# Sums of the message layer with nodes on the partitions, and a rectifier taken inside an addition

## The chip, the cores and the metric

The kernel runs on one core of one Trainium2 chip. The metric is the device time of one execution in microseconds (us); smaller is better. Runs of the kernel before and of the changed kernel are compared by their medians.

The engines of a core are named as in the profile: PE is TensorE (matrix products), PEld its weight loads, DVE is VectorE, ACT is ScalarE, POOL is GpSimd, SP is SyncE, which here only issues DMA transfers.

## What is computed

A graph transformer layer over 1250 nodes with 512 features and 21250 edges. Its branches are a graph message layer, linear attention and a feed-forward part with eight experts. The change touches the message layer, in the reference:

```python
m = jnp.maximum(jnp.max(weighting_gate), jnp.float32(0.0))
exp_e = jnp.exp(weighting_gate - m)
row_sum = jax.ops.segment_sum(exp_e, src, num_segments=n_nodes)
atten_e = exp_e / (row_sum[src] + 1e-06)
Mfeat = source_features @ Wm + bm
out0 = jax.ops.segment_sum(atten_e[:, None] * Mfeat[dst], src, num_segments=n_nodes)
out1 = jax.ops.segment_sum(atten_e[:, None] * Mfeat[src], dst, num_segments=n_nodes)
message_feats = jnp.concatenate([out0, out1], axis=-1)
h = message_feats @ W1 + b1
h = jax.nn.relu(_layernorm(h, gamma, beta))
h = jax.nn.relu(h @ W2 + b2)
valid = (row_sum > 0)[:, None]
return jnp.where(valid, h, jnp.float32(0.0))
```

and around it:

```python
xn = _layernorm(x, axis=-1)
x = x + gnn(xn, ...) + mix(xn[None], ...)[0]
x = x + ffn(_layernorm(x, axis=-1)[None], ...)[0]
```

## The kernel before

The 1250 nodes are 10 tiles of 125 nodes (`NT`, `TP`); two tiles form a window of 250 nodes (`WIN`), of which there are five (`NW`). The program is written by hand for each engine: every engine has its own list of instructions and semaphores between them, and nothing reorders them.

The stages in order of time: loads and edge sorting beside the projections of all tiles (to about 150 us), attention output and more sorting (to 225 us), the dense weighted adjacency matrix built from the sorted edges (L731, L739 on PE, L1646 on ACT, to 312 us), the message layer (312.6 to some 392 us), routing to the experts (to 410 us), and 17 chunks of the expert layer (to the end).

Wm and W1 are folded ahead, so `msg` holds for each node 256 values: 128 for the sum outwards (columns 0 to GH) and 128 for the sum inwards (GH to MD), both of them already in the 128 features of h. `adjw` holds the adjacency in float32, node of a tile t on the partitions, the other node in windows along the free axis.

**First loop of the message layer** (t over 10 tiles). `adj_turn` turns the ten 125x125 blocks of tile t on PE (L751), ACT copies the result as the rounded part `adjT_hi` (L1654) and DVE takes the rest as `adjT_lo` (L1297). Then `inward(t)` (L758) adds, for each of the five windows, `msg[:, t, GH:MD]` (loaded as weights, 128 columns) times `adjw` (streamed, 250 columns) into `hid_at(w)`. These are float32 products. The result stands with the 128 features on the partitions and nodes along the free axis.

**Second loop** (w over 5 windows). `outward(w, half)` (L781 to L783) adds for each of ten source tiles j three products in the type float32r: `out_hi` or `out_lo` as weights (128 columns), 250 columns of `adjT_hi` or `adjT_lo` streamed, into `hid_to(w)`. ACT copies both sums to SBUF (`hid_in` L1667, with the bias b1, and `hid_copy` L1675), PE turns them so that nodes are on the partitions (`hid_turn`, L793 and L794), and DVE scales the outward part with 1/row_sum and adds the inward part (`hid_var`, L1323 and L1326), takes mean and variance, and normalises (`hid_norm`, L1343). PE turns the result back (`hid_back`, L802), ACT applies gamma, beta and the rectifier (L1686), PE multiplies with W2 (`hid_out`, L809, one product for each tile), DVE adds b2 (`upd_bias`, L1351), ACT applies the rectifier and the mask of valid nodes (`relu`, L1691), DVE adds the result to the residual stream `rec` (`x1_norm`, L1356) and takes its statistics. PE turns `rec` (`x2_turn`, L817), ACT copies it (L1697), PE computes the router's scores (`route`, L824, 8 columns streamed).

In each list the steps of different windows are interleaved by hand. DVE's list after the first loop is, for w from 1 to 7: `hid_var(w-1)`, `x1_norm`, `hid_norm(w-1)`, `x1_norm`, two `upd_bias`; so the sums of the last window stand behind `upd_bias` of tiles 4 and 5 there.

SP waits for the last outward sum (`hid_ps`), then issues in this order: four pieces of the experts' second weights (L462, 1 MB each), half of the first weights (L463, 2 MB), their bias (L464, 2 MB), the ten tiles of `rec` as they become ready (L398, 2.56 MB in all) and last the factors of every row (L470). POOL gathers the rows for the experts (L507) after all of that has been written.

Of the kernel before, what the change touches and what calls it, by code (L numbers as in the profile page):

```python
# [13 lines left out]
ALU = mybir.AluOpType  # L14
# [20 lines left out]
WIN = 250  # L35
# [76 lines left out]
def build(nc, x, edge_src, edge_dst, edge_w, consts, halves, biases, small, fold, wqkv, wp, bvt, w1f, w2f, b2f, out):  # L112
    with ExitStack() as ctx:
# [107 lines left out]
        hidc = place("hidc", 26064, [128, 2, WIN])  # L221
        hido = place("hido", 40664, [128, 2, WIN])
# [49 lines left out]
        valid = sb("valid", [TP, NT])  # L272
# [36 lines left out]
        def hid_at(w):  # L309

            return bank[3 + w][:, 0:WIN]

        def hid_to(w):

            return bank[3 + w][:, 256:256 + WIN]
# [9 lines left out]
        def piece(a, i):  # L325
# [51 lines left out]
        hidi_ok, comb_ok = sem("hidi_ok"), sem("comb_ok")  # L377
        hid_ps, hidc_ok, hn_ps, hvar_ok, hstd_ok, hn_ok, hT_ps, hidT_ok, upd_ps, upd_ok, relu_ok, x1_ok = (
            sem("hid_ps"), sem("hidc_ok"), sem("hn_ps"), sem("hvar_ok"), sem("hstd_ok"), sem("hn_ok"), sem("hT_ps"),
            sem("hidT_ok"), sem("upd_ps"), sem("upd_ok"), sem("relu_ok"), sem("x1_ok"))  # L380
# [35 lines left out]
        def _(sp):  # L416
# [43 lines left out]
            sp.wait_ge(hid_ps, NW)  # L460
            for i in range(4):
                sp.dma_start(piece(w2_raw, i), piece(w2f, i)).then_inc(ld_w2k[i], 16)  # L462
# [63 lines left out]
        def _(pe):  # L526
# [1333 lines left out]
```

## Time and profile before

| | us |
|---|---|
| median of 3 runs | 494.15 (493.7 to 494.18) |
| the profiled execution, its time | 493.5 |
| the profiled execution, first to last instruction (span) | 491.4 |
| first loop of the message layer | 312.6 to 344.7 |
| second loop up to the last outward sum | 344.7 to 371.6 |
| from there to the first gather of the experts' rows | 371.6 to 405.5 |

Over the whole span PE is busy for 86%, its weight loads for 70%, DVE 75%, ACT 61%, POOL 40%; the mean granted clock of PE is 0.959 of full speed. Of the chain that ended last, PE has 64% of the span.

How to read it: times in the trace are us from the first instruction. In a row of instructions the name before the arrow is written, those after it are read (streamed operand first, loaded weights second), then rows and columns of the weights, then rows and columns streamed. A float32 product that is no turn leaves two records, one for each pass over its columns; a turn and a float32r product leave one (both types are shown as f32). Records of PE overlap, so what one costs in a stream is the distance between two starts, or the time of a group in the chain of work divided by its count; the mean ns of one is its latency.

### The profile page before, as it was taken

How to read it: one execution, taken by the hardware profiler on the slowest of the kernel's cores; microseconds unless marked ns; L12 is line 12 of the kernel's file. 1: busy time of each engine (PE TensorE's matmuls, PEld its weight loads, DVE VectorE, ACT ScalarE, POOL GpSimd, SP SyncE). 2: the span in 40 equal slices, each digit the busy share in tenths (PEclk: the TensorE clock that was granted, in tenths of full speed). 3: DMA queues.
4: the chain of work that ended last, by engine and by line, in shares of the span. 5: the costliest groups of instructions: out<-in, count | busy, mean ns of one | idle time of the engine just before them, and what ended most of it. 6: DMA issues, size and time to landing. Idle time of an engine off the chain costs nothing.

```text
span 491.4 us, 8811 instructions
## 1 busy us (share of the span) xinstructions
PE 424.5 (86%) x2701; PEld 343.4 (70%) x2701; DVE 366.9 (75%) x717; ACT 298.3 (61%) x845; POOL 194.8 (40%) x160
## 2 busy tenths in 40 slices
PE   3665999999999999999777777899898957999992
PEld 1454887888887788877555555799876746788881
DVE  6786688877786888698999998478279874455552
ACT  4577999988897123363777777554335662666550
POOL 0378878688887787870000000000000008254321
PEclk9878999999999999999999999999999858999998
DMA  7992000000000000005000000000006964243210
GB/s 228 284 250 49 1 3 3 1 4 2 3 3 1 2 2 3 2 3 191 2 1 2 1 2 0 3 1 0 1 1 258 412 225 128 74 120 110 68 65 16
DMA packets 15742, 31.07 MB, mean 63 GB/s; under 512 B 7652, under 2 KB 8283, under 8 KB 14675
## 3 DMA queue, kind: packets, MB, share of 16 engines
q1 hardware_dynamic: 9266, 23.21, 14.6%
q0 software_dynamic: 6432, 7.31, 7.5%
q8 instruction: 24, 0.39, 0.3%
q14 instruction: 20, 0.16, 0.1%
HBM read 24.90 MB, written 7.37 MB: 66 GB/s over the span
## 4 chain that ended last, share of the span: by engine, by line
PE 64%; ACT 14%; DVE 10%; issue 6%; DMA 3%; POOL 1%; SPq 1%; ACTq 0%; DVEq 0%; POOLq 0%
PE banks L569 25%; PE banks L739 9%; PE banks L892 7%; PE banks L758 4%; ACT adj L1646 4%; PE banks L751 2%; ACT q_sb L1580 2%; PE banks L824 2%; PE banks L650 2%; PE banks L883 2%; ACT k_sb L1580 1%; DVE chunk_1h L1214 1%; DMA x_rows<-factors 1%; ACT q_sb L1563 1%; PE banks L731 1%
## 5 line engine op out<-in xcount | busy, mean ns | idle before, releaser
L496 POOL DMA_INDIRECT slots<-record,row_i x116 | 153.7, 1325 | 40.7 <-issue 40.7
L507 POOL DMA_INDIRECT rec<-x_rows,get_i x17 | 18.7, 1098 | 190.7 <-DMA x_rows<-factors 185.8
L1646 ACT ACTIVATE adj<-banks x108 | 58.4, 588 | 27.9 <-PE banks L739 26.8
L569 PE MATMUL banks<-w_hi,xT_hi 128*125 128x512 f32 (+1 forms) x160 | 61.5, 385 | 5.7 <-DVE xT_lo L1085 5.7
L739 PE MATMUL banks<-d_hot,s_hot 128*128 128x251 f16 x432 | 60.0, 276 | 0.2
L569 PE MATMUL banks<-w_lo,xT_hi 128*125 128x512 f32 (+1 forms) x160 | 60.1, 375 | 0.0
L569 PE MATMUL banks<-w_hi,xT_lo 128*125 128x512 f32 (+1 forms) x160 | 60.0, 375 | 0.0
L569 PEld LDWEIGHTS banks<-w_hi,xT_hi 128*125 128x125 f32 x160 | 30.9, 193 | 12.0 <-issue 6.1
L739 PEld LDWEIGHTS banks<-d_hot,s_hot 128*128 128x128 f16 x432 | 33.5, 98 | 7.5 <-issue 0.7
L569 PEld LDWEIGHTS banks<-w_lo,xT_hi 128*125 128x125 f32 x160 | 30.9, 193 | 5.8
L569 PEld LDWEIGHTS banks<-w_hi,xT_lo 128*125 128x125 f32 x160 | 30.6, 191 | 6.1
L516 POOL DMA_INDIRECT out<-o_sb,out_i x17 | 17.1, 1005 | 40.9 <-DVE o_sb L1462 40.9
L1268 DVE TENSOR_TENSOR d_hot<-col,keys 128x2000 f16<-128x2000 f16 (+1 forms) x28 | 32.3, 1153 | 0.0
L731 PE MATMUL banks<-hlf 128*128 128x1 f16 x108 | 18.3, 170 | 16.1 <-ACT adj L1646 16.1
L1276 DVE TENSOR_TENSOR s_hot<-s_one,parts 128x2048 f16<-128x2048 f16 x26 | 31.6, 1215 | 0.0
L1457 DVE TENSOR_TENSOR y_sb<-banks,b_sb 128x512 f32<-128x512 f32 x17 | 11.8, 691 | 26.2 <-PE banks L569 26.2
L731 PEld LDWEIGHTS banks<-hlf 128*128 128x128 f16 x108 | 10.4, 96 | 28.9 <-issue 26.9
L1580 ACT ACTIVATE q_sb<-q_sb,hmax 125x64 f32<-125x64 f32 x80 | 26.7, 335 | 4.3 <-DVE hmax L1113 4.2
L1609 ACT ACTIVATE row_1h<-row_one,sort_f 125x128 f16<-125x128 f16 x54 | 19.7, 432 | 13.8 <-DVE row_one L1208 8.0
L1580 ACT ACTIVATE k_sb<-k_sb,hmax 125x64 f32<-125x64 f32 x80 | 26.6, 333 | 0.0
L702 PE MATMUL banks<-chunk_1h,row_1h 125*128 125x216 f16 x216 | 22.8, 258 | 3.2 <-DVE chunk_1h L1214 2.2
L1617 ACT ACTIVATE xT_hi<-banks 128x500 fp32r<-128x500 f32 x10 | 5.9, 588 | 30.6 <-PE banks L663 30.6
(297 smaller groups left out, 1083.1 us busy)
## 6 DMA issues: line engine op xcount, KB each, us to landing
w_raw<-in_w2f SPq DMA_DIRECT2D x4, 1024.0 KB, 8.1
w_raw<-in_wqkv SPq DMA_DIRECT2D x3, 1024.0 KB, 15.2
x_rows<-rec SPq DMA_DIRECT2D x10, 224.0 KB
w1a<-in_w1f SPq DMA_DIRECT2D x1, 2048.0 KB, 7.8
w1b<-in_w1f SPq DMA_DIRECT2D x1, 2048.0 KB, 16.5
b_sb<-in_b2f SPq DMA_DIRECT2D x1, 2048.0 KB, 22.9
slots<-record,row_i POOLq DMA_INDIRECT x116, 2.6
rec<-in_x SPq DMA_DIRECT2D x1, 1120.0 KB
```

Source lines behind the costliest of these rows:

```text
L496: pool.indirect_dma_start(slots, bass.IndirectOffsetOnAxis(ap=row_i[:, c:c + 1], axis=0), record[:, c, :], None).then_inc(slot_st, 16)
L569: mm = pe.matmul(dst, ab, cd, start=(i == 0), stop=(i == n - 1))
L702: mm = pe.matmul(bank[1 - v // 2][:, v % 2 * NCH:(v % 2 + 1) * NCH], row_1h[:, n % RS, v, :, j], chunk_1h[:, n % RS, :, j], start=(n == 0 ...
L731: pe.matmul(flat_banks[:, bass.ds(at_new, 1)], before, zero_col, start=True, stop=False, skip_group_check=True)
L739: mm = pe.matmul(flat_banks[:, bass.ds(at_in, AW)], s_hot[:, n % DB, i, q, :, j], d_hot[:, n % DB, q, :, j], start=False, stop=(i == WT - ...
L758: mm = pe.matmul(hid_at(w), msg[:, t, GH:MD], adjw[:, t, w, 0:WIN], start=(t == 0), stop=(t == NT - 1), skip_group_check=True)
L892: mm = pe.matmul(bank[1][:, 0:F], xsT[:, c % 2, k, :], w1_sb[k // 2][:, k % 2, bass.ds(e * F, F)], start=(k == 0), stop=(k == KD - 1))
L1268: dve.tensor_tensor(d_hot[:, r, 0:k, 0:WIN, :], col_2[:, :, :].unsqueeze(1).to_broadcast([128, k, WIN, 2]), of_keys(1).to_broadcast([128, ...
L1276: last = dve.tensor_tensor(s_hot[:, r, :, :, :, :], s_one[:, n % 2, :, :, :].unsqueeze(1).to_broadcast(shape), both.unsqueeze(3).to_broadc ...
L1580: last = act.activation(ah, ah, ACT.Exp, bias=hmax[:, i, h:h + 1], accum_out=hsum[:, i, h:h + 1])
L1609: last = act.activation(row_1h[:, n % RS, VD, :, j], row_one[:, n % 2, :, j], ACT.Copy, scale=sort_f[:, 2 * n + j:2 * n + j + 1])
L1646: act.activation(adj[:, bass.ds(w, BW2)], flat_banks[0:TP, bass.ds(out_at, BW2)], ACT.Copy).then_inc(win_ok, 1)
```

## The change

The operands of the two sums change places. The adjacency blocks are loaded as weights (125 columns) and the 128 features of the messages are streamed, so the sums stand with nodes on the partitions. Their copies in that layout (`hidc`, `hido`) and the turns of `hid_turn` go. The bias b1, which stood on the partitions, is put in by ten small products at the start of the first loop (`in_bias`: b1 spread over 125 weight columns, the identity streamed). DVE takes the outward sum straight from PSUM, scales it and adds the inward sum in one instruction for each tile; the inward sums are copied by ACT to a new tile `hin`. `hin` lies where the second and third quarter of the experts' second weights are to go, so SP waits for the last use of it before pieces 1 to 3. The mask of valid nodes becomes an addend (0, or -3e38 for a node that is not valid) in `upd_bias`, and the rectifier is taken by DVE as a maximum with 0 in the addition to `rec`; ACT's `relu` goes.

```diff
@@ tiles and places in PSUM
-        hidc = place("hidc", 26064, [128, 2, WIN])
-        hido = place("hido", 40664, [128, 2, WIN])
+        hin = place("hin", 10240, [TP, NW, 2, GH])
-        def hid_at(w):
-            return bank[3 + w][:, 0:WIN]
-        def hid_to(w):
-            return bank[3 + w][:, 256:256 + WIN]
+        def in_at_of(n):
+            return bank[3 + n // 2][0:TP, n % 2 * MD:n % 2 * MD + GH]
+        def out_at_of(n):
+            return bank[3 + n // 2 if n >= 2 else 0][0:TP, n % 2 * MD + GH:(n % 2 + 1) * MD]
@@ SP
-            sp.wait_ge(hid_ps, NW)
+            sp.wait_ge(hid_ps, NT)
             for i in range(4):
+                if i == 1:
+                    sp.wait_ge(comb_ok, NW)
                 sp.dma_start(piece(w2_raw, i), piece(w2f, i)).then_inc(ld_w2k[i], 16)
@@ PE
+            def in_bias(n):
+                pe.matmul(in_at_of(n), little("g1").to_broadcast([128, TP]), ident, start=(n % 2 == 0), stop=False,
+                          skip_group_check=True)
             def inward(t):
-                for w in range(NW):
-                    mm = pe.matmul(hid_at(w), msg[:, t, GH:MD], adjw[:, t, w, 0:WIN], start=(t == 0),
-                                   stop=(t == NT - 1), skip_group_check=True)
+                for n in range(NT):
+                    mm = pe.matmul(in_at_of(n), adjw[:, t, n // 2, n % 2 * TP:(n % 2 + 1) * TP], msg[:, t, GH:MD],
+                                   start=False, stop=(t == NT - 1), skip_group_check=True)
...
+                if t == 0:
+                    pe.wait_ge(ld_small, 16)
+                    for n in range(NT):
+                        in_bias(n)
...
-            def outward(w, half_):
-                if w >= 1 and half_ == 0:
-                    pe.wait_ge(hidi_ok, w)
-                for j in range(5 * half_, 5 * half_ + 5):
-                    cols = slice(w * WIN, (w + 1) * WIN)
-                    pe.matmul(hid_to(w), out_hi[:, j, :], adjT_hi[:, j, cols], start=False, stop=False, skip_group_check=True)
-                    pe.matmul(hid_to(w), out_hi[:, j, :], adjT_lo[w][:, j, :], start=False, stop=False, skip_group_check=True)
-                    mm = pe.matmul(hid_to(w), out_lo[:, j, 0:GH], adjT_hi[:, j, cols], start=False,
-                                   stop=(j == NT - 1), skip_group_check=True)
+            def outward(n):
+                cols = slice(n * TP, (n + 1) * TP)
+                if n >= 2:
+                    pe.wait_ge(hin_ok, n // 2 + 1)
+                low = slice(n % 2 * TP, (n % 2 + 1) * TP)
+                for j in range(NT):
+                    pe.matmul(out_at_of(n), adjT_hi[:, j, cols], out_hi[:, j, :], start=(n == 0 and j == 0), stop=False, skip_group_check=True)
+                    pe.matmul(out_at_of(n), adjT_hi[:, j, cols], out_lo[:, j, 0:GH], start=False, stop=False,
+                              skip_group_check=True)
+                    mm = pe.matmul(out_at_of(n), adjT_lo[n // 2][:, j, low], out_hi[:, j, :], start=False,
+                                   stop=(j == NT - 1), skip_group_check=True)
...
-            def hid_turn(w):
...
@@ DVE
-            dve.tensor_scalar(valid[:, :], rs[:, :], 0.0, None, ALU.is_gt)
+            dve.tensor_scalar(shut[:, :], rs[:, :], 0.0, -3e38, ALU.is_le, ALU.mult)
             def hid_var(w):
-                dve.wait_ge(hn_ps, w + 1)
+                dve.wait_ge(hid_ps, 2 * w + 2)
+                dve.wait_ge(hin_ok, w + 1)
                 for i in range(2):
-                    t = 2 * w + i
-                    last = dve.tensor_scalar(comb[:, w % 2, i, :], bank[0][0:TP, (2 + i) * GH:(3 + i) * GH], rinv[:, t:t + 1], None,
-                                             ALU.mult)
-                own_step(last)
-                dve.tensor_tensor(comb[:, w % 2, :, :], comb[:, w % 2, :, :],
-                                  bank[0][0:TP, 0:2 * GH].rearrange("p (i n) -> p i n", i=2), ALU.add).then_inc(comb_ok, 1)
+                    n = 2 * w + i
+                    last = dve.scalar_tensor_tensor(comb[:, w % 2, i, :], out_at_of(n), rinv[:, n:n + 1], hin[:, w, i, :], ALU.mult,
+                                                    ALU.add)
+                last.then_inc(comb_ok, 1)
...
-                dve.tensor_tensor(upd[:, t % 2, :], upd_at(t), bias("g2"), ALU.add).then_inc(upd_ok, 1)
+                dve.scalar_tensor_tensor(upd[:, t % 2, :], upd_at(t), shut[:, t:t + 1], bias("g2"), ALU.add,
+                                         ALU.add).then_inc(upd_ok, 1)
...
-                dve.wait_ge(relu_ok, t + 1)
-                dve.tensor_tensor(rec[:, t, :], rec[:, t, :], upd[:, t % 2, :], ALU.add).then_inc(x1_ok, 1)
+                dve.wait_ge(upd_ok, t + 1)
+                dve.scalar_tensor_tensor(rec[:, t, :], upd[:, t % 2, :], 0.0, rec[:, t, :], ALU.max,
+                                         ALU.add).then_inc(x1_ok, 1)
@@ ACT: hid_copy and relu go, and
             act.wait_ge(in_ps, 1)
-            hid_in(1).then_inc(hidi_ok, 1)
-            hid_copy(0)
+            for w in range(NW):
+                hid_in(w)
```

On PE the first loop stood like this before (turns L751, inward sums L758; `cst` is the table with the identity):

```order
L751 MATMUL banks<-cst,adj 125x125 x10
L758 MATMUL banks<-adj,msg 128x250 x5
L751 MATMUL banks<-cst,adj 125x125 x10
L758 MATMUL banks<-adj,msg 128x250 x5
```

and stands like this now (turns L752, bias L758, inward sums L764):

```order
L752 MATMUL banks<-cst,adj 125x125 x10
L758 MATMUL banks<-cst,sml 125x128 x10
L764 MATMUL banks<-msg,adj 125x128 x10
L752 MATMUL banks<-cst,adj 125x125 x10
L764 MATMUL banks<-msg,adj 125x128 x10
```

Each tile has ten inward products instead of five, and the first tile ten for the bias ahead of them.

At the end of the second loop on PE, before: the last outward products of window 4, then the products with W2 for tiles 4 and 5 (L809), the turn back (L802), the turns of `hid_turn` for window 4, and the scores of tiles 0 and 1 (L824).

```order
L781 MATMUL banks<-adjT_hi,out_hi 128x250
L782 MATMUL banks<-adjT_lo_90,out_hi 128x250
L783 MATMUL banks<-adjT_hi,out_lo 128x250
L809 MATMUL banks<-sml,hidT 125x512 x2
L802 MATMUL banks<-cst,hid 128x125 x2
L793 MATMUL banks<-cst,hidc 125x128
L794 MATMUL banks<-cst,hido 125x128
L793 MATMUL banks<-cst,hidc 125x128
L794 MATMUL banks<-cst,hido 125x128
L824 MATMUL banks<-sml,x2T 125x8 x8
```

Now, at the same place (outward products L792, L793, L795; the product with W2 is L811, the turn back L804, the scores L826):

```order
L792 MATMUL banks<-out_hi,adjT_hi 125x128
L793 MATMUL banks<-out_lo,adjT_hi 125x128
L795 MATMUL banks<-out_hi,adjT_lo_90 125x128
L811 MATMUL banks<-sml,hidT 125x512 x2
L804 MATMUL banks<-cst,hid 128x125 x2
L826 MATMUL banks<-sml,x2T 125x8 x8
```

The triples of outward products were 50 in all and are now 100; the turns are gone, and what follows keeps its order.

On SP, with what each transfer waits for, before:

```order
L462 DMA w_raw<-in_w2f 128x2048 [waits hid_ps]
L462 DMA w_raw<-in_w2f 128x2048 x3
L463 DMA w1b<-in_w1f 128x4096
L464 DMA b_sb<-in_b2f 128x4096
```

and now:

```order
L463 DMA w_raw<-in_w2f 128x2048 [waits hid_ps]
L463 DMA w_raw<-in_w2f 128x2048 [waits comb_ok]
L463 DMA w_raw<-in_w2f 128x2048 x2
L464 DMA w1b<-in_w1f 128x4096
L465 DMA b_sb<-in_b2f 128x4096
```

The second piece, and with it all that SP issues after it, now waits for `comb_ok`, which DVE raises with the sums of the last window.

## Rows read from the trace of the kernel before

**Rows 1.** Busy time by stage: us, busy us (instructions) by engine, clock, DMA share, GB/s.

```profile
312.60:344.70 32.10, 32.08 (x201) 29.93 (x201) 25.14 (x50) 14.54 (x31) 0.00 (x0) 1.00 0.00 1
344.70:371.60 26.90, 24.77 (x191) 22.22 (x190) 15.45 (x49) 10.84 (x23) 0.00 (x0) 1.00 0.01 1
...
374.80:400.50 25.70, 20.05 (x127) 16.23 (x126) 21.50 (x61) 15.63 (x22) 0.00 (x0) 0.78 1.02 398
```

**Rows 2.** Chain that ended last, first loop: start us, us, engine, line, count.

```profile
316.10 1.09 PE banks L751 x10
317.19 2.12 PE banks L758 x10
```

**Rows 3.** Timelines of PE and DVE, second loop: start, latency, instruction, count, [idle before].

```profile
345.17 0.28 PE L781 MATMUL banks<-adjT_hi,out_hi 125*128 125x250 f32 x1
...
350.06 0.27 PE L793 MATMUL banks<-cst,hidc 128*125 128x128 f32 x1
...
350.77 0.61 DVE L1323 TENSOR_SCALAR comb<-banks,rinv 125x128 f32<-125x128 f32 x2 [5.72 <-PE banks L794]
...
353.86 0.43 PE L802 MATMUL banks<-cst,hid 125*128 125x125 f32 x2 [1.45 <-DVE hid L1343]
...
366.52 0.43 PE L802 MATMUL banks<-cst,hid 125*128 125x125 f32 x2 [0.68 <-DVE hid L1343]
```

**Rows 4.** SP issuing the second weights; then their times to landing (L462).

```profile
371.78 1.98 SPq L462 DMA_DIRECT2D w_raw<-in_w2f  x4
...
DMA to landing us min/median/max: 5.0/8.1/11.1
```

**Rows 5.** Stages of 1 us; columns as in rows 1.

```profile
382.00:383.00 1.00, 1.00 (x9) 1.00 (x9) 0.81 (x3) 0.86 (x2) 0.00 (x0) 0.71 1.00 426
...
400.00:401.00 1.00, 0.00 (x0) 0.00 (x0) 0.90 (x5) 1.00 (x2) 0.00 (x0) 0.50 0.79 229
```

**Rows 6.** Chain of work behind the routing.

```profile
398.25 6.43 DMA x_rows<-factors
...
405.47 4.23 DMA rec<-x_rows,get_i
```

**Rows 7.** Timelines of PE and DVE around and behind the last outward sum.

```profile
369.19 0.61 DVE L1323 TENSOR_SCALAR comb<-banks,rinv 125x128 f32<-125x128 f32 x2
...
371.58 1.88 PE L809 MATMUL banks<-sml,hidT 128*125 128x512 f32 x4
...
374.72 1.27 DVE L1351 TENSOR_TENSOR upd<-banks,bia 125x512 f32<-125x512 f32 x2
375.91 0.60 DVE L1323 TENSOR_SCALAR comb<-banks,rinv 125x128 f32<-125x128 f32 x2
376.54 0.42 DVE L1326 TENSOR_TENSOR comb<-comb,banks 125x256 f32<-125x256 f32 x1
...
380.03 0.43 PE L802 MATMUL banks<-cst,hid 125*128 125x125 f32 x2 [1.57 <-DVE hid L1343]
```

**Rows 8.** Chain of work: scores of two tiles, twice; turns of an expert chunk.

```profile
380.46 1.65 PE banks L824 x16
...
392.30 3.24 PE banks L824 x16
...
424.24 0.44 PE banks L883 x4
```

**Rows 9.** Groups by line and shape, 310 to 420 us: busy us, mean ns | idle before.

```profile
L758 PEld LDWEIGHTS banks<-adj,msg 125*128 125x128 f32 x100 | 18.2, 190 | 1.7
...
L781 PEld LDWEIGHTS banks<-adjT_hi,out_hi 125*128 125x128 f32 x50 | 9.4, 189 | 0.0
```

**Rows 10.** Timeline of PE in the attention part.

```profile
59.99 0.69 PE L604 MATMUL banks<-v_sb,k_sb 125*64 125x65 f32 x16
60.61 0.65 PE L560 MATMUL banks<-cst,xn 125*128 125x125 f32 x4
```

More of the change, by code:

```diff
@@ L271, in build @@
         rinv = sb("rinv", [TP, NT])
-        valid = sb("valid", [TP, NT])
+        shut = sb("shut", [TP, NT])
         ws_sum = sb("ws_sum", [TP, E])
@@ L376, in build @@
             sem("out_split"))
[L377 to L380, printed above, removed]
+        hin_ok, comb_ok = sem("hin_ok"), sem("comb_ok")
+        hid_ps, hvar_ok, hstd_ok, hn_ok, hT_ps, hidT_ok, upd_ps, upd_ok, x1_ok = (
+            sem("hid_ps"), sem("hvar_ok"), sem("hstd_ok"), sem("hn_ok"), sem("hT_ps"),
+            sem("hidT_ok"), sem("upd_ps"), sem("upd_ok"), sem("x1_ok"))
         var2_ok, std2_ok, x2T_ps, x2T_ok, log_ps, log_ok, lexp_ok, route_ok, route_ps = (
@@ L773, in _ @@
             ws = little("ws").rearrange("p (k e) -> p k e", k=KD)
[L775 to L795 removed]
+            def outward(n):
[8 more added lines that the diff above has]
+                    mm = pe.matmul(out_at_of(n), adjT_lo[n // 2][:, j, low], out_hi[:, j, :], start=False,
+                                   stop=(j == NT - 1), skip_group_check=True)
+                mm.then_inc(hid_ps, 1)
             def hid_back(w):
@@ L835, in _ @@
             for w in range(NW):
-                outward(w, 0)
-                if w >= 1:
-                    hid_turn(w - 1)
+                outward(2 * w)
                 if w == NW - 1:
                     both(x2_turn, 0)
-                outward(w, 1)
+                outward(2 * w + 1)
                 if w >= 2:
@@ L845, in _ @@
                     hid_back(w - 1)
-            hid_turn(NW - 1)
             both(route, 0)
@@ L1664, in hid_in @@
             def hid_in(w):
-                if w >= 2:
-                    act.wait_ge(hn_ps, w - 1)
-                return act.activation(hidc[:, w % 2, :], hid_at(w), ACT.Identity, bias=little("g1"))
-            def hid_copy(w):
-                act.wait_ge(hid_ps, w + 1)
-                if w == 0:
-                    hid_in(0)
-                if w >= 2:
-                    act.wait_ge(hn_ps, w - 1)
-                act.activation(hido[:, w % 2, :], hid_to(w), ACT.Copy).then_inc(hidc_ok, 1)
+                act.activation(hin[:, w, :, :], bank[3 + w][0:TP, :].rearrange("p (i a) -> p i a", i=2)[:, :, 0:GH],
+                               ACT.Copy).then_inc(hin_ok, 1)
             def hid_std(w):
@@ L1687, in hid_relu @@
                                scale=little("gamma")).then_inc(hidT_ok, 1)
-            def relu(t):
-                act.wait_ge(upd_ok, t + 1)
-                act.activation(upd[:, t % 2, :], upd[:, t % 2, :], ACT.Relu, scale=valid[:, t:t + 1]).then_inc(relu_ok, 1)
             def x2_copy(t):
@@ L1709, in _ @@
             act.wait_ge(in_ps, 1)
-            hid_in(1).then_inc(hidi_ok, 1)
-            hid_copy(0)
+            for w in range(NW):
+                hid_in(w)
             for w in range(1, NW):
-                if w + 1 < NW:
-                    hid_in(w + 1).then_inc(hidi_ok, 1)
                 if w == NW - 1:
@@ L1717, in _ @@
                 hid_std(w - 1)
-                hid_copy(w)
                 if w == NW - 1:
                     hid_relu(w - 1)
-                if w >= 2:
-                    both(relu, w - 2)
                 if w < NW - 1:
@@ L1727, in _ @@
             hid_relu(NW - 1)
-            both(relu, NW - 2)
             both(x2_copy, 2)
-            both(relu, NW - 1)
             both(x2_copy, 3)
```

9 lines of the change are left out of this document (removed).

## The prediction, made before the changed kernel ran

> **What bounds the kernel now.** I read the busy time by stage first. In the first loop of the message layer PE is busy 32.08 of 32.10 us, in the second 24.77 of 26.90 us up to the last outward sum; DVE has 25.14 and 15.45 us there, ACT 14.54 and 10.84 [rows 1]. So PE sets both loops, and a nanosecond added to each product is paid in full. Then the chain that ended last: one tile of the first loop is 1.09 us of turns and 2.12 us of inward sums, ten times over, with nothing between [rows 2]. Then PE's timeline in the second loop: from 345.17 to 350.06 there are 42 outward products, so they start 0.1165 us apart, and all 150 take 17.5 us; PE idles twice for DVE, 1.45 and 0.68 us [rows 3].
>
> Behind the last outward sum another thing rules. At 371.78 SP begins to issue the experts' weights [rows 4], and from then on the DMA engines carry some 11 MB (8 MB of weights and bias, 2.56 MB of rows): from 374.8 to 400.5 their share is 1.02, at 398 GB/s [rows 1]. The stream thins out only after 400 [rows 5]. The factors are issued at 398.25, stand behind it, and land 6.43 us later; the gather and the expert layer start from there [rows 6]. So this part ends not when DVE and PE have the routing, but when the stream that began at the last outward sum has drained. DVE and PE have about 2 us to spare.
>
> **The change part by part.** T is the end of the last outward product on PE, 371.58 before [rows 7].
>
> *Inward sums.* Per tile 5 x 250 streamed columns become 10 x 128, in two passes each. Before, ten records took 2.12 us, 0.212 each; by columns a pass over 128 is 0.109 [rows 2]. Four turns over 128 columns took 0.44 us, 0.110 each [rows 8]. Twenty passes at 0.110 are 2.2 us, 0.08 more for each tile: +0.8 us.
>
> *Bias.* Ten products of 128 columns in two passes, 20 x 0.110 = +2.2 us. They stand on PE between turns and sums of the first tile, in a loop where PE never waits [rows 1], so nothing hides them.
>
> *Outward sums.* This is the large term. 150 products that stream 250 columns become 300 that stream 128. The streamed columns stay the same but for 2%, yet every product has its own weight load, and the number of loads doubles. The trace shows a load for each record even where the weights repeat: L758 uses one block of weights for five windows and has 100 loads for its 100 records [rows 9]. How fast can loads follow one another? The scores (L824) load 125 columns for every 8 streamed: 16 in 1.65 us, 0.103 each [rows 8]; nothing but the load can take that. The turns of the first loop load the very adjacency blocks and stream 125 columns: 0.109 each [rows 2], so load and stream overlap. The load for a float32r product has the latency of one for float32, 189 and 190 ns [rows 9], so I take it to be the same work. The new products stream for some 0.06 us (128/250 of 0.1165) under a load of 0.103. I put them between 0.103 and 0.109, at 0.106: 300 x 0.106 = 31.8 us against 17.5, +14.3 us. Ends of the unknown: 0.163 (0.103 + 0.060) if load and stream of short float32r products do not overlap; 0.076 if loads are as quick as the attention's products with 64 weight columns suggest, 16 in 0.62 us or 0.038 each, doubled [rows 10]; 0.060 if only the stream counted.
>
> *Turns.* 16 of the 20 turns of `hid_turn` stand before T: four groups like the 0.44 us of rows 8, -1.75 us. The last group is off the path.
>
> *Stalls.* PE's waits of 1.45 and 0.68 us are for `hid_norm` [rows 3]. A window now takes PE at least 60 x 0.106 = 6.4 us, while the way from sums to `hid_norm` took 353.86 - 350.77 = 3.1 us. They go, -2.1 us. Next late would be DVE, whose round for a window took 375.91 - 369.19 = 6.7 us [rows 7], and which saves 0.4 us of it (two instructions of 0.3 for 0.60 and 0.42). PE has 6.4 us of sums, 1.7 of products with W2 (L809) and 0.2 of turns in each round, so it is never behind DVE.
>
> *ACT.* Five copies of 256 columns come in a row after the first loop; DVE's instruction of that size takes 0.42 us [rows 7], so ACT's may take as much, 2 us in all. PE needs them only for the third outward tile, 6.4 us later. Nil. The removed copies and `relu` stood beside PE's work, and behind T in the slack named above. Nil.
>
> *The new wait on SP.* Pieces 1 to 3, and all that SP issues behind them, wait for DVE's sums of the last window. In DVE's list `upd_bias` of tiles 4 and 5 stands ahead, and that needs L809, which PE makes right after T: 1.88 us, then 0.64 for the second `upd_bias` and 0.60 for the two sums [rows 7]. That makes T + 3.2; SP issues at T + 3.4 instead of T + 0.7. Meanwhile piece 0 occupies the DMA engines. The first piece landed 5.0 us after its issue, the last, issued some 1.6 us later, 11.1 us after its own [rows 4]: 2.5 us for each. Piece 1 landed near T + 7.7 and can now land at T + 3.4 + 5.0 = T + 8.4. So the stream is late by 0.7 us; by 0 if piece 1 starts up wholly under piece 0, by 2.7 us if nothing hides. I take +0.7, nearest to the landing times.
>
> *Routing.* DVE reaches the last window's sums at T + 2.6 instead of T + 4.3 [rows 7] and is 2 to 3 us nearer to T with the factors. By the stream that is worth nothing. The clock fell to half after 382 [rows 5], and of two equal groups of scores the one at 392.30 took 3.24 us instead of 1.65 [rows 8]; that too lies in the slack. If this slack were not there, up to 2 us would be gained.
>
> Sum: 0.8 + 2.2 + 14.3 - 1.75 - 2.1 + 0.7 = +14.15 us. On the profiled execution's 493.5 that gives 507.65; the median of the runs stands 0.65 above it, so 508.3.
>
> **A rule against this, weighed.** The chain shows 0.103 for a load with 8 streamed columns [rows 8]. The Trainium skill, "TensorE: Matmul & The Clock Gate", section "Back-to-back issue gap", gives about 81 ns for each product of a stream of loads and products at 128 columns. By it the outward sums would take an estimated 24.3 us and the total would be near 500.8. For this type the trace disagrees. The same page, Part 3, says that a load overlaps a running product only when their row groups differ; here they would then not overlap, which is the third rival below. The 0.109 of a turn that both loads and streams 125 columns [rows 2] disagrees with that as well.
>
> **Rivals.**
> *Quicker loads.* 0.076 each, 9 us less: 499.3. For it: L604's 0.038 for 64 columns [rows 10]. Against: those products write the two halves of the array in turn and may overlap each other, and the scores' weights have the same shape as the new ones.
> *No slower than before.* If loads cost nothing and only the stream counted, PE would pay 0.0595 x 300 = 17.9 us for the outward sums, and 0.8 + 2.2 + 0.4 - 1.75 - 2.1 + 0.7 = +0.25; with 128 columns at the rate of a float32 pass (0.109 for two columns' time each, 0.055) it is 16.4 us and -1.3: 492.9. The time turns at 0.0587 for a product. Against it stands every row with a load in it, and PE's stalls would stay, with windows as short as before.
> *No overlap.* 0.163 each, 17.1 us more: 525.4. For it: no row shows float32r with so short a stream. Against: the turns.
> *Clock.* PE streams for only half of the outward stage. If the granted clock fell to 1.2 GHz as it did behind 382 [rows 5], a load would take twice as long, as in rows 8: +31.8, 540. Against: that fall came behind 1.57 us of idle [rows 7] and behind scores that stream only 8 columns; here there is neither.
>
> **How the numbers follow.** Forecast 0.71, its own spread 505 to 512.5 (0.103 to 0.116 for a product, 0 to 2.7 for the stream). Quicker loads 0.10 (499 to 505), no slower than before 0.06, no overlap 0.07, clock 0.04, rest 0.02. The range holds the first two: 499 to 512.5. A measurement of this kernel tells about 0.2% (1 us) from no change: faster 0.04, within that 0.02, slower 0.94.
>
> **What would show it.** In the profile after: a first loop 3.0 us longer, 3.29 us a tile; outward products 0.106 us apart at full clock; no idle of PE for DVE before T; T near 385; the last window's sums done 3.2 us behind T; the gather again behind the factors' landing, whose issue has moved nearer to T while the landing has not; nothing changed from the gather to the end. A distance of 0.08 or 0.16 between outward starts would make the forecast wrong, and so would a gather much nearer to T than 34.6 us (405.47 - 371.58 [rows 6, 7], plus 0.7).

## The result, and the profile after

| | kernel before | changed kernel |
|---|---|---|
| median, 4 runs each | 493.92 us (492.47 to 494.18) | 508.56 us (506.73 to 511.79) |
| profiled execution: time | 493.5 | 509.01 |
| span | 491.4 | 506.9 |

The ratio is 1.0312, 95% interval 1.0278 to 1.0346: 14.6 us slower by the medians. The forecast was 508.3, range 499 to 512.5, so time, direction and size came as forecast. What follows is whether they came for the reasons given.

The versions further down ran on other chips, each beside runs of the kernel before (medians 495.26, 492.9 and 493.28 us), and their ratios are to those. Executions in a slower state, such as one of the last version with 595.35 us at a mean granted clock of 0.682, count in no ratio.

First the busy time by stage of the changed kernel (us; then busy us and count of PE, PEld, DVE, ACT, POOL; granted clock; DMA share; GB/s). The stages are the first loop, the second loop to the last outward sum (T), and T to the gather.

```profile
312.70:347.90 35.20, 35.20 (x323) 35.20 (x323) 25.48 (x50) 14.54 (x31) 0.00 (x0) 1.00 0.00 1
347.90:385.30 37.40, 37.40 (x323) 35.37 (x321) 16.84 (x52) 6.59 (x15) 0.00 (x0) 1.00 0.01 1
385.30:420.10 34.80, 28.31 (x169) 23.19 (x169) 30.61 (x77) 15.99 (x20) 0.01 (x1) 0.75 0.85 316
```

Against [rows 1] PE is now busy for all of both loops, its loads for nearly all, and its clock is full. The chain of work shows the first loop (start, us, count): the bias, then 1.09 and 2.19 us for a tile, where [rows 2] has 1.09 and 2.12.

```profile
314.02 2.19 PE banks L758 x20
316.20 2.19 PE banks L764 x20
318.39 1.09 PE banks L752 x10
319.48 2.19 PE banks L764 x20
```

PE's timeline in the second loop, where [rows 3] has products every 0.1165 us (column two is a record's latency):

```profile
347.98 0.27 PE L792 MATMUL banks<-out_hi,adjT_hi 125*125 125x128 f32 x1
348.09 0.27 PE L793 MATMUL banks<-out_lo,adjT_hi 125*125 125x128 f32 x1
...
350.27 0.28 PE L792 MATMUL banks<-out_hi,adjT_hi 125*125 125x128 f32 x1
```

21 products stand between 347.98 and 350.27: 0.109 each, 32.8 us for 300. The groups by line and shape show a load for every record, of the same latency as before [rows 9]:

```profile
L792 PEld LDWEIGHTS banks<-out_hi,adjT_hi 125*125 125x125 f32 x100 | 18.9, 189 | 0.0
```

Behind T, SP's timeline with its four pieces of the stream:

```profile
385.49 4.36 SPq L463 DMA_DIRECT2D w_raw<-in_w2f  x4
```

and DVE's timeline:

```profile
386.41 1.61 DVE L1349 SCALAR_TENSOR_TENSOR upd<-banks,shut,bia 125x512 f32<-125x512 f32 x2 [0.94 <-PE banks L811]
387.93 0.60 DVE L1323 SCALAR_TENSOR_TENSOR comb<-banks,rinv,hin 125x128 f32<-125x128 f32 x2
```

DVE's last window sums end at 388.53, 3.2 us behind T, and SP's four pieces stretch over 4.36 us instead of 1.98 [rows 4]. The chain then, where [rows 6] has 6.43 us and the gather at 405.47:

```profile
412.50 6.82 DMA x_rows<-factors
...
420.09 4.08 DMA rec<-x_rows,get_i
```

So the profiled spans differ like this (T is 371.58 and 385.30):

| stretch | before | after | difference | forecast |
|---|---|---|---|---|
| start to first loop | 312.62 | 312.69 | +0.1 | 0 |
| first loop | 32.4 | 35.2 | +2.8 | +3.0 |
| second loop to T | 26.6 | 37.4 | +10.8 | +10.45 |
| T to the gather | 33.9 | 34.8 | +0.9 | +0.7 |
| gather to the end | 85.9 | 86.8 | +0.9 | 0 |
| sum | 491.4 | 506.9 | +15.5 | +14.15 |

One sign came otherwise than forecast: the factors are issued 27.2 us behind T (412.50) and not nearer to it than before (398.25, 26.7 us behind). The section on SP's wait comes back to it.

### The profile page after: what moved, and what is told of

It is laid out like the page before. It is cut to its first block, busy times and chain, and to the rows that moved or that the text cites. A ratio compares the mean times of both kernels' runs of the same rounds, so it can differ in the third digit from the quotient of the medians.

```text
span 506.9 us, 9288 instructions
## 1 busy us (share of the span) xinstructions
PE 439.8 (87%) x2951; PEld 361.0 (71%) x2951; DVE 365.7 (72%) x712; ACT 290.0 (57%) x830; POOL 192.6 (38%) x160
## 4 chain that ended last, share of the span: by engine, by line
PE 66%; ACT 13%; issue 6%; DVE 5%; SPq 4%; DMA 3%; POOL 1%; ACTq 0%; DVEq 0%; POOLq 0%
PE banks L570 24%; PE banks L740 9%; PE banks L891 6%; PE banks L764 4%; SPq L397 4%; ACT adj L1646 4%; PE banks L752 2%; PE banks L793 2%; PE banks L795 2%; PE banks L792 2%; ACT q_sb L1580 2%; PE banks L882 2%; PE banks L651 2%; ACT k_sb L1580 1%; DMA x_rows<-factors 1%
## 5 line engine op out<-in xcount | busy, mean ns | idle before, releaser
L508 POOL DMA_INDIRECT rec<-x_rows,get_i x17 | 17.0, 998 | 205.3 <-DMA x_rows<-factors 200.4
L1646 ACT ACTIVATE adj<-banks x108 | 58.5, 589 | 27.8 <-PE banks L740 26.7
L570 PEld LDWEIGHTS banks<-w_hi,xT_hi 128*125 128x125 f32 x160 | 30.6, 191 | 14.5 <-issue 8.6
L740 PEld LDWEIGHTS banks<-d_hot,s_hot 128*128 128x128 f16 x432 | 33.5, 98 | 7.5 <-issue 0.7
L570 PEld LDWEIGHTS banks<-w_hi,xT_lo 128*125 128x125 f32 x160 | 30.4, 190 | 6.0
L1457 DVE TENSOR_TENSOR y_sb<-banks,b_sb 128x512 f32<-128x512 f32 x17 | 11.8, 692 | 26.7 <-PE banks L570 26.7
L1580 ACT ACTIVATE q_sb<-q_sb,hmax 125x64 f32<-125x64 f32 x80 | 26.7, 336 | 4.3 <-DVE hmax L1112 4.2
L792 PE MATMUL banks<-out_hi,adjT_hi 125*125 125x128 f32 x100 | 27.4, 274 | 0.0
L795 PE MATMUL banks<-out_hi,adjT_lo 125*125 125x128 f32 x100 | 27.2, 272 | 0.0
L793 PE MATMUL banks<-out_lo,adjT_hi 125*125 125x128 f32 x100 | 27.2, 272 | 0.0
## 6 DMA issues: line engine op xcount, KB each, us to landing
w1b<-in_w1f SPq DMA_DIRECT2D x1, 2048.0 KB, 14.5
```

The costliest lines, as they stand in the source:

```text
L570: mm = pe.matmul(dst, ab, cd, start=(i == 0), stop=(i == n - 1))
L740: mm = pe.matmul(flat_banks[:, bass.ds(at_in, AW)], s_hot[:, n % DB, i, q, :, j], d_hot[:, n % DB, q, :, j], start=False, stop=(i == WT - ...
L792: pe.matmul(out_at_of(n), adjT_hi[:, j, cols], out_hi[:, j, :], start=(n == 0 and j == 0), stop=False, skip_group_check=True)
L793: pe.matmul(out_at_of(n), adjT_hi[:, j, cols], out_lo[:, j, 0:GH], start=False, stop=False, skip_group_check=True)
L795: mm = pe.matmul(out_at_of(n), adjT_lo[n // 2][:, j, low], out_hi[:, j, :], start=False, stop=(j == NT - 1), skip_group_check=True)
L1580: last = act.activation(ah, ah, ACT.Exp, bias=hmax[:, i, h:h + 1], accum_out=hsum[:, i, h:h + 1])
```

## What sets the distance of the outward products

The theory is that the weight load sets it; its rival, that the short float32r stream does. Two versions of the changed kernel halve one of the two. The first leaves out the outward sums of the nodes 64 to 124 of each tile:

```diff
-                cols = slice(n * TP, (n + 1) * TP)
+                cols = slice(n * TP, n * TP + 64)
-                low = slice(n % 2 * TP, (n % 2 + 1) * TP)
+                low = slice(n % 2 * TP, n % 2 * TP + 64)
-                    pe.matmul(out_at_of(n), adjT_hi[:, j, cols], out_hi[:, j, :], ...
+                    pe.matmul(out_at_of(n)[0:64, :], adjT_hi[:, j, cols], out_hi[:, j, :], ...
```

and the same for the other two products.

> The changed kernel, with only 64 of the 125 weight columns loaded in each outward product (the outward sums of the nodes 64 to 124 of each tile are left out); 128 columns are still streamed. The outward products started 0.109 us apart in the changed kernel. Theory (the load sets this distance): 64 columns load in about half the time, so the starts come down to 0.06 to 0.08 us, and 300 products are 9 to 15 us shorter: 494 to 500 us. Rival (the stream sets it, float32r streaming 128 columns at the rate of a float32 pass, 0.109): the distance stays 0.109 and the time stays near 508.5.

PE's timeline:

```profile
350.51 0.22 PE L792 MATMUL banks<-out_hi,adjT_hi 125*64 125x128 f32 x1
...
352.32 0.22 PE L792 MATMUL banks<-out_hi,adjT_hi 125*64 125x128 f32 x1
```

30 products lie between these two rows, 0.060 us each. With half the weight columns and all 128 columns streamed the distance falls from 0.109 to 0.060. So the load set it, and a float32r stream of 128 columns takes 0.060 or less. That is close to the break-even of the prediction, 0.0587, and from the first loop to SP's first piece this kernel takes 58.4 us (313.7 to 372.05), the kernel before 59.2. The time is 498.09 us, 1.0059 of the kernel before (1.0011 to 1.0106): what it loses lies behind that point (35.6 us to the gather and 88.5 to the end, for 33.7 and 85.9), where other sums are routed. That wasn't followed up.

The second version leaves out half of the features of the outward sums:

```diff
-                    pe.matmul(out_at_of(n), adjT_hi[:, j, cols], out_hi[:, j, :], ...
+                    pe.matmul(out_at_of(n)[:, 0:64], adjT_hi[:, j, cols], out_hi[:, j, 0:64], ...
```

> The changed kernel, with only 64 of the 128 columns streamed in each outward product (half of the features of the outward sums are left out); 125 weight columns are loaded as before. Theory (load sets the distance): 0.103 to 0.109 us between starts, at most 2 us less in all, 506.5 to 508.5. Rival (the stream sets it): the stream is halved, and the distance would fall to the load's 0.103 as well if load and stream overlap, so this run alone does not part the two; but if load and stream were served one after the other (0.109 = load + part of the stream), it would fall below 0.09 and the time below 503.

Neither came: 538.54 us. PE's timeline, and the stages around the place (columns as above):

```profile
354.55 0.27 PE L795 MATMUL banks<-out_hi,adjT_lo 125*125 125x64 f32 x1
354.66 0.27 PE L792 MATMUL banks<-out_hi,adjT_hi 125*125 125x64 f32 x1
354.77 0.31 PE L793 MATMUL banks<-out_lo,adjT_hi 125*125 125x64 f32 x1
354.89 0.40 PE L795 MATMUL banks<-out_hi,adjT_lo 125*125 125x64 f32 x1
355.10 0.40 PE L792 MATMUL banks<-out_hi,adjT_hi 125*125 125x64 f32 x1
355.31 0.40 PE L793 MATMUL banks<-out_lo,adjT_hi 125*125 125x64 f32 x1
```

```profile
350.00:354.00 4.00, 4.00 (x39) 4.00 (x39) 0.65 (x2) 2.77 (x6) 0.00 (x0) 1.00 0.02 4
354.00:356.00 2.00, 2.00 (x16) 2.00 (x15) 0.00 (x0) 0.00 (x0) 0.00 (x0) 0.72 0.00 0
356.00:380.00 24.00, 24.00 (x116) 24.00 (x116) 4.23 (x18) 1.15 (x3) 0.00 (x0) 0.50 0.00 1
```

Up to 354.8 the products stand 0.109 us apart (14 of them from 353.24 to 354.77), with half the stream: the load again, and not load and stream one after the other. Then the granted clock falls to 1.2 GHz and the distance becomes 0.21. PE is busy without a gap, and so are its loads; what is less than in the changed kernel is only the columns streamed. This is what the prediction's fourth rival, given 0.04 and priced with +31.8, had feared. The version takes 30 us more than the changed kernel, 24.5 of them from the first loop to SP's first piece (97.3 us for 72.8); with 128 columns the fall doesn't happen.

## The bias products

```diff
-                if t == 0:
-                    pe.wait_ge(ld_small, 16)
-                    for n in range(NT):
-                        in_bias(n)
...
-                                   start=False, stop=(t == NT - 1), ...
+                                   start=(t == 0 and n % 2 == 0), stop=(t == NT - 1), ...
```

> The changed kernel without the ten bias products (the bias b1 is left out); the first inward product of each bank starts the sum. Theory: they stand uncovered on PE, 2.2 us; the first loop and the whole are 2.2 us shorter, 506.3. Rival (the wait for the first scaled messages stands behind them and takes their place): at most 0.5 us is gained, 508.

Measured 508.98 us, ratio to before 1.0289 (1.0211 to 1.0367). The interval is wider than the effect, so the stage decides: from the first loop's start to SP's first piece 70.7 us (313.1 to 383.8) instead of 72.8. The 2.1 us are there and uncovered, though the whole doesn't show them. In its chain the inward sums follow the turns at once:

```profile
313.11 1.33 PE banks L752 x10
314.44 2.22 PE banks L764 x20
```

## What sets the gather

The prediction said that behind T the DMA stream is the bound, not routing. Three kernels tell that. The first loads 2 MB more:

```diff
             sp.dma_start(b2_sb[:, :], b2f.partition_broadcast(128)).then_inc(ld_b2, 16)
+            sp.dma_start(spare[:, :], b2f.partition_broadcast(128)).then_inc(ld_b2, 16)
```

> The kernel before with 2 MB more in the stream behind T (the experts' output bias is loaded a second time, into a region that is free then). Theory (the stream sets the gather): 2 MB at some 420 GB/s are 5 us, the gather comes 5 us later and the whole takes 499, up to 1 us more for a colder clock. Rival (routing sets it, the stream is cover): the first 2 us are free and the gather comes at most 3 us later, 497; if the stream had more slack, nothing changes.

498.29 us, ratio 1.0103 (1.0034 to 1.0172). From SP's first piece to the gather it takes 39.3 us (370.4 to 409.7) instead of 33.7: 2 MB cost 5.6 us in full. More of routing ran at half clock in this execution, so the factors were also issued later (30.0 us behind SP's first piece for 26.5); but the list of rows stood ready at 406.0, 3.7 us ahead of the gather. The factors took 8.50 us to land instead of 6.43. The stream is the bound, not routing.

The second takes the rectifier's part of the change alone, on the kernel before:

```diff
-                dve.tensor_tensor(upd[:, t % 2, :], upd_at(t), bias("g2"), ALU.add).then_inc(upd_ok, 1)
+                dve.scalar_tensor_tensor(upd[:, t % 2, :], upd_at(t), shut[:, t:t + 1], bias("g2"), ALU.add,
+                                         ALU.add).then_inc(upd_ok, 1)
...
-                dve.tensor_tensor(rec[:, t, :], rec[:, t, :], upd[:, t % 2, :], ALU.add).then_inc(x1_ok, 1)
+                dve.scalar_tensor_tensor(rec[:, t, :], upd[:, t % 2, :], 0.0, rec[:, t, :], ALU.max,
+                                         ALU.add).then_inc(x1_ok, 1)
```

> The kernel before with the second part of the change alone: mask as an addend, rectifier as a maximum in DVE's addition, no rectifier on ACT; the sums as before. Theory (behind T the DMA stream sets the end): T and the gather stay where they were, 0 within 0.5 us: 493.9. Rival (the chain over DVE and ACT sets it): two waits of 0.2 us and the hand-overs go, 1 to 2 us less, 492 to 493.

494.05 us, ratio 1.0016 (0.9979 to 1.0054): no change that can be told, with 33.5 us from SP's first piece to the gather, although the factors were written 1.2 us sooner against that piece. The rectifier's part of the change costs nothing that can be told; what the change costs comes with the new sums.

The third is the changed kernel with the load of the output bias issued behind the factors:

```diff
-            sp.dma_start(b2_sb[:, :], b2f.partition_broadcast(128)).then_inc(ld_b2, 16)
             for t in range(NT):
...
                          factors[:, :, :]).then_inc(fac_st, 16)
+            sp.dma_start(b2_sb[:, :], b2f.partition_broadcast(128)).then_inc(ld_b2, 16)
```

> The changed kernel with the load of the experts' output bias (2 MB) issued behind the factors instead of ahead of the rows. Theory: the stream ahead of the factors is 5 us shorter; the gather's list of rows is ready 5.3 us ahead of the gather in the changed kernel, so the gather comes nearly 5 us sooner. PE's warm-up products, which run until about 36 us behind T, then end behind it and hold back the first turns, so 3.5 of it are left: 505 (504 to 506). Rival (the rows' own small transfers set it, not the bytes ahead): no change, 508.5.

502.2 us, ratio to before 1.0168 (1.0111 to 1.0225), a larger gain than I had expected. The profile is of the slowest of the four executions (505.24 us). In it SP's first piece to gather is 31.3 us instead of 34.6. The list of rows is written at 417.1 and the gather starts at 418.1, so there routing has become the bound.

## What SP's new wait costs

Here the copies of the inward sums go where the inward half of the messages lies dead, and the wait goes.

```diff
-        hin = place("hin", 10240, [TP, NW, 2, GH])
-                if i == 1:
-                    sp.wait_ge(comb_ok, NW)
-                    ... rinv[:, n:n + 1], hin[:, w, i, :], ALU.mult,
+                    ... rinv[:, n:n + 1], msg[:, n, GH:MD], ALU.mult,
-                act.activation(hin[:, w, :, :], ...
+                act.activation(msg[:, 2 * w:2 * w + 2, GH:MD], ...
```

> The changed kernel with the copies of the inward sums written over the inward half of the messages, which is dead by then; SP's wait for the last window's sums goes. Theory: the stream of the experts' weights starts 0.9 us sooner against T and, since that stream sets when the gather starts, the gather comes 33.9 instead of 34.8 us behind T: 507.7. Rival (the stream makes a late start good, or something else sets the gather): the stretch from T to the gather stays 34.8 and the time 508.5.

510.73 us, ratio 1.0323 (1.0245 to 1.0401), no gain. SP's first piece to gather is 34.7 us, as long as with the wait. To see how steady this stretch is, both kernels were profiled again, unchanged.

> The kernel before, unchanged, for its stages on this chip: first loop to T 59.0 to 59.2 us, T to the gather 33.7 us. If the second stretch differs from 33.7 by half a microsecond, the 0.9 us by which it is longer in the changed kernel can't be read from one profile.

> The changed kernel, unchanged, for its stages on this chip. If SP's wait costs 0.9 us, T to the gather is that much longer than in the kernel before on the same chip; the run with the copies moved (34.7 us without the wait) says that it costs nothing, and then the two should differ by less than the same kernel does between profiles.

They took 494.95 and 508.31 us. The stretch by kernel:

| kernels | SP's first piece to the gather, us |
|---|---|
| sums as before (the first profile, again, with the new rectifier, with wide scores) | 33.7, 33.6, 33.5, 33.4 |
| new sums with SP's wait (the first profile, again, without bias) | 34.6, 35.0, 35.2 |
| new sums, no wait on SP | 34.7 |

The extra microsecond comes back in every profile, but the wait is not shown to be its cause. About half of it can be placed. In the kernel before, SP is done with the rows at 396.78 and issues the factors at 398.25, as soon as DVE has written them. In the changed kernel DVE has written them at 408.6, but SP still issues rows, the longest of these issues 5.14 us:

```profile
374.79 21.99 SPq L398 DMA_DIRECT2D x_rows<-rec  x20
```

```profile
391.00 21.45 SPq L397 DMA_DIRECT2D x_rows<-rec  x20
412.50 0.53 SPq L471 DMA_DIRECT2D x_rows<-factors  x1
```

So the factors leave 27.0 us behind SP's first piece instead of 26.5, and take 6.82 us to land instead of 6.43. Without the wait they leave at 26.65 and take longer still. The stages from 28 to 30 us behind SP's first piece, in the changed kernel and in the one without the wait:

```profile
413.50:415.50 2.00, 2.00 (x11) 1.68 (x8) 1.93 (x6) 1.03 (x2) 0.00 (x0) 0.50 0.82 252
```

```profile
412.50:414.50 2.00, 1.15 (x12) 1.07 (x13) 1.86 (x10) 1.97 (x3) 0.00 (x0) 0.50 0.67 162
```

In the kernel before this stage moved 171 GB/s. So without the wait the bulk of the stream drains some 0.45 us sooner (90 GB/s for 2 us, at an estimated 400), about as soon as in the kernel before. But the factors' own transfer, issued at 411.15, takes 7.29 us there against 6.43 in [rows 6] and the gather gains nothing. With the sums as before the factors land 32.6 to 32.9 us behind SP's first piece, with the new sums 33.8 to 34.5, with or without the wait. What makes this longer stays open.

## The clock behind T, and a version that beats both

Moving the output bias in the kernel before as well, with the new rectifier and 8 warm-up products (`MOE_UP`) instead of 12, should have gained 1 us.

> The kernel before, with the second part of the change, the load of the output bias behind the factors, and 8 warm-up products instead of 12. Theory: in the kernel before the list of rows is ready only 1 us ahead of the gather, so moving 5 us of stream out of the way gains 1 us: 493. Rival (factors set it by their own 2 us of slack, or the later bias collides with the gathers): nothing, or 1 us slower.

493.9 us, ratio 1.0009 (0.9973 to 1.0045). The chain of work of the profiled execution, which was the slowest of the ten (497.25 us):

```profile
386.62 3.41 PE banks L809 x4
...
392.85 3.10 PE banks L824 x16
395.94 1.76 PE banks L817 x8
397.71 3.38 PE banks L824 x16
...
410.20 4.96 DMA rec<-x_rows,get_i
```

In it routing sets the gather, and runs mostly at half clock: the turns of `x2_turn` take 1.76 us for two tiles where they take 0.87 at full clock, the last four tiles' scores 3.10 and 3.38 for 1.65 [rows 8]. The gather comes 36.7 us behind SP's first piece. In the kernel before the stream had covered what routing lost at half clock. How much of this the other nine executions had isn't shown, and so neither is why the median gained nothing.

With half of the stream the clock had fallen although PE never idled, so the few columns of the scores may be what lowers it here. They are 8 under a load that takes 0.103 us, so more columns should be free. In the next kernel the router's weights are streamed twelve times over:

```diff
-                    mm = pe.matmul(bank[6][0:TP, t * E:(t + 1) * E], x2T[:, t % 2, k, :], ws[:, k, :],
+                    mm = pe.matmul(scores[0:TP, t // 5, t % 5, :, :], x2T[:, t % 2, k, :],
+                                   ws[:, k, :].unsqueeze(1).to_broadcast([128, REP, E]),
```

> The kernel before, with the router's weights streamed twelve times over in each score product (96 columns instead of 8, the copies land in unused columns of PSUM). Theory (the clock falls where PE streams few columns, and the load of 0.103 us covers up to some 100 columns of a float32 pass): the scores keep 1.65 us for two tiles, the clock stays at 2.4 GHz through the scores from 386 us on, and the last two tiles take 1.65 instead of 3.24 us; routing is done 1.6 us sooner. The whole stays within 0.5 us, since the DMA stream sets the gather. Rival (only idle time lowers the clock): the last scores still run at half clock.

493.54 us. PE's timeline at the last scores, in this kernel and in the unchanged one on the same chip:

```profile
384.13 1.88 PE L827 MATMUL banks<-sml,x2T 128*125 128x96 f32 x16
...
391.16 1.99 PE L827 MATMUL banks<-sml,x2T 128*125 128x96 f32 x16 [0.25 <-ACT x2T L1703]
```

```profile
390.43 1.91 PE L824 MATMUL banks<-sml,x2T 128*125 128x8 f32 x16 [0.25 <-ACT x2T L1697]
...
393.50 3.52 PE L824 MATMUL banks<-sml,x2T 128*125 128x8 f32 x16 [0.25 <-ACT x2T L1697]
```

Twelve times the columns cost 1.99 instead of 1.91 us, and the last group doesn't fall to half clock. PE idled no less (1.20 and 0.25 us ahead of the last two groups, in the unchanged kernel 0.25 and 0.25), so idle time alone isn't what lowered the clock. This is one execution, but in the profiles with 8 columns the last group took 3.15 us or more each time, and the next version, with 96, has 1.99 again. The list of rows is ready 30.4 us behind SP's first piece instead of 32.1; the whole is unchanged, since the stream is the bound there.

The last kernel puts these together on the sums of the kernel before.

> The kernel before, with the second part of the change (mask and rectifier on DVE), the wide scores, the experts' output bias loaded behind the factors, three products that fill PE's idle time of 1.6 us ahead of the last turn back, the split of the first piece of the second weights moved behind routing, and 10 warm-up products. Theory: with the stream 5 us shorter and the clock kept up, routing sets the gather, and it comes 2.5 to 4 us sooner than in the kernel before; 490 to 491.5. Rival (the gather is held by the rows' own small transfers, or the moved splits delay the first expert chunk): 493 to 494.

488.01 us, ratio 0.991 (0.9874 to 0.9945): faster than both. By the interval it gains 2.7 to 6.2 us on the kernel before, where 2.5 to 4 had been expected. What each of its parts gives wasn't measured. Its chain of work:

```profile
389.93 2.00 PE banks L827 x16
...
400.10 0.18 DVE get_i L1453
...
401.11 4.93 DMA rec<-x_rows,get_i
...
409.17 1.99 PE banks L898 x8
```

The gather comes 30.3 us behind SP's first piece instead of 33.7, right behind `get_i`. And the first expert chunk runs at full clock, 1.99 us. In the changed kernel it doesn't:

```profile
424.26 0.82 ACT xs L1725
...
425.21 0.64 PE banks L882 x4
...
427.31 3.78 PE banks L891 x8
431.08 0.87 PE banks L882 x4
```

Routing came sooner, so the warm-up products ended sooner against the gather. PE then idled 3.6 us, and the first chunk's turns and products ran longer at half clock (3.78 and 0.87 us; the kernel before has 3.53 and 0.60 there). Of the last 0.9 us of the table above this is only a part: at the end of the third group of turns the changed kernel is 0.3 us later against the gather. The other 0.6 us stands at the very end, where the last products with the second weights take 2.27 us, in the kernel before 1.67:

```profile
496.93 2.27 PE banks L570 x6
```

Neither is steady. In the second profile of the kernel before the first chunk took 1.99 us and the last products 2.89. In the changed kernel's second profile they took 3.77 and 2.76, and PE idled 3.9 us ahead of the chunk. PE's idling ahead of the chunk may make the difference there, but the first profile of the kernel before has 3.53 us behind only 0.73 us of it, and no version tested it.

## Why the prediction was right, step by step

- *PE sets both loops*: right. It is now busy for 72.6 of 72.6 us.
- *Inward sums +0.8 and bias +2.2*: right. 2.19 instead of 2.2 us for twenty passes; the first loop is 2.8 us longer, and the bias alone is 2.1 by its removal.
- *Outward sums +14.3*: right in mechanism, a little small. 0.109 and not 0.106 for a product, 32.8 us, +15.3. The turns of the first loop, which have that very distance, were the better row; the scores' 0.103 was not reached even with 64 columns streamed (0.109). That the load is the bound is shown by halving it, and that it overlaps the stream by halving the stream.
- *Turns -1.75, stalls -2.1*: both stalls are gone, as PE's full busy time shows. With +15.3 for the sums these would leave +11.4 for the second loop; +10.8 was measured. The starts in PE's timelines place the 0.6 us. Taken to the start of what follows, and without idle time, the groups of outward products took 18.4 us before and 32.9 now, +14.5, since a group of 15 behind turns had taken 1.82 to 1.85 us and not 1.75; the four groups of turns took 1.5 us and not 1.75. The changes from one kind of product to the next, which the sum had not listed, cost more in the kernel before.
- *SP's wait +0.7*: the wait ends where it was forecast (sums done 3.2 us behind T), and the stretch is 0.9 us longer, but without the wait it stays longer. The size was right and the cause is not shown. The sign given for it, factors issued nearer to T, came the other way (27.2 us for 26.7), because SP was still issuing rows when they were written; nothing in the prediction had looked at how long SP takes for that.
- *The stream covers the gains behind T*: right. Routing came 3.3 us sooner against T (the list of rows stood ready 28.7 instead of 32.0 us behind it), the rectifier alone changes nothing, and 2 MB more cost 5.6 us. The slack in the kernel before was smaller than the 2 us I gave: the list of rows is written at 403.6 and the gather starts at 405.47, with 0.75 us of issue between, which leaves about 1 us.
- *Nothing changes from the gather to the end*: wrong by 0.9 us. About 0.3 stands at the first chunk, behind warm-up products whose end is tied to routing and not to the gather; I had not looked at what stands behind a chain that becomes earlier. The other 0.6, at the last products, moves as much between two profiles of the kernel before (1.67 and 2.89 us).
- *Quicker loads (499.3)*: refuted. The page of the Trainium skill weighed there, "TensorE: Matmul & The Clock Gate", section "Back-to-back issue gap", gives 81 ns at 128 columns; here it is 109 ns with 125 weight columns and 60 ns with 64. The rule of the same page's "Part 3: Packing small matmuls", by which a load overlaps a running product only in another row group, isn't what these products show: 109 ns is about the load alone (103 ns in the scores), and half the stream leaves it at 109.
- *No overlap (525.4)*: refuted by the same distances. *No slower than before (492.9)*: its break-even of 0.0587 holds roughly, as the half load shows with 0.060, but loads weren't free.
- *Clock (540)*: didn't happen with 128 streamed columns, but did with 64 in a version without any idling, which the prediction had not thought of.
- *The forecast's own spread*: its terms (0.103 to 0.116 for a product, 0 to 2.7 us for the stream) give 506.7 to 513.3 and not 505 to 512.5. The measured 508.56 lies in either.

That 508.3 and 508.56 lie so close is partly luck: +1.0 us was too little for the products, +0.9 behind the gather and -0.6 in the second loop were missed, and single runs of the changed kernel spread over 5 us.

## What to carry to other kernels

Swapping the operands of the products here left the streamed columns nearly as they were (150 x 250 became 300 x 128) but doubled the weight loads: count products times weight columns against streamed columns, and put the operand on the streaming side that lets one load serve the more columns. Here four groups of turns of 0.44 us were saved against 150 more loads of 0.109. Before you cost an edit at nothing because something else ends last, look at what runs at a lower clock or waits in that slack: it becomes the bound as soon as the cover is shortened.

## What the runs showed that I had not expected

- With loads back to back and PE busy all the time the granted clock fell to 1.2 GHz when products streamed 64 columns per 0.109 us, and stayed at 2.4 GHz with 128 per 0.109 us. The Trainium skill, "TensorE: Matmul & The Clock Gate", section "HAM oscillation — how this bites in real kernels", tells of gaps in which PE idles; here there was none. The cost was 24.5 us by the time to SP's first piece (97.3 against 72.8).
- At the scores streaming more columns under the same load was nearly free and kept the clock up: 96 columns instead of 8 cost 0.08 us in 1.91 and saved 1.5 at the last scores (1.99 for 3.52), in the two profiles that have them.
- Float32r products with 64 weight columns stand 0.060 us apart, with 125 columns 0.109, with the same 128 columns streamed: between these two the time goes by weight columns.
